# A feed-forward layer whose transposes move to transfers, and whose first token group is held back to the end

## The chip, the cores and the metric

The kernel runs on all 8 cores of one Trainium2 chip. Each core takes one of the 8 sequences (4096 tokens of 1024 features), and the cores don't exchange anything. The metric is the device time of the slowest core in microseconds. A core has TensorE (PE) for matmuls, VectorE (DVE), ScalarE (ACT) and GpSimd (POOL) for the rest, and SyncE (SP), whose queue issues nearly all transfers here. Each engine works through its own instructions in the order in which the program lists them, and waits for the others by semaphores.

## The reference, cut to what matters

```python
x = x + layernorm(attn(layernorm(x)))   # a selective scan over time, state 256
x = x + layernorm(ffn(layernorm(x)))

def ffn(x):                              # x: tokens x 1024
    h = bit_linear(x, w1)                # activations to 8 bits by token, weights to -1, 0, 1; 1024 -> 4096
    h = conv1d(h, conv_w, pad=(1, 1)) + conv_b   # depthwise over time, 3 taps
    h = silu(h)
    return bit_linear(h, w2)             # again quantized by token; 4096 -> 1024
```

Every token's row is divided by its own largest magnitude and rounded before each of the two linear layers. The second quantization needs the maximum over all 4096 hidden features of a token, so W2 of a token can only begin when all its hidden features are there.

## The kernel before, in words

A first phase (to about 310 us) computes the attention half for 32 groups of 128 tokens and stores its result x2 in memory. The change lies in the second phase, the FFN.

The FFN runs over `NF` = 8 tiles of 512 tokens, each with 32 chunks of 128 hidden features. The loop over `n` goes through 256 such chunks (slot `n`, tile `f1 = n // 32`, slot of the tile `s1 = n % 32`), and in the same pass W2 follows `LAG` + 32 = 38 slots behind: `m = n - 38` is a quarter of the hidden features' pieces of a tile, in steps of 4 chunks by 128 tokens. So a slot holds eight W1 matmuls for chunk `n` (`w1_mm`, line 721) and eight W2 matmuls for piece `m` (`w2_mm`, line 850); eight pieces make one output group `Gx`, of which there are 32 (`NG`), each accumulated in one of two PSUM pairs. The program order of the loop is written out by hand, and is the order on each engine. Slots 0 to 37 have no W2, slots 256 on have no W1.

Per chunk ScalarE evacuates W1's result to `hp` (`evac`, L727) and computes one tap (`tap1`, L746) and, for two chunks at once, SiLU (`silu`, L772). VectorE does the other taps (`conv0` L753, `conv2` L760, `conv1` L765), running maxima (`minmax`, L780) and, for the tile before, the multiply and round of one piece (`quant_mul` L833, `quant_rnd` L839), one slot ahead of the W2 that reads the piece. The hidden values live in a ring `h4` of 72 chunks. At the start of a tile the maxima are combined, transposed on TensorE, turned into scales and broadcast (`absmax_comb`, `absmax_T` L797, `scales`, `bcast` L817 and L820).

Beside this the input groups of the next tile are normalized and quantized, one group each eight slots, by the slot's remainder `r`: GpSimd centres (`ln3_center`, L406), ScalarE squares and VectorE takes the maximum (L411), small instructions follow, ScalarE scales (L435), and VectorE writes the rounded bf16 rows `xqmB` (`quant_x`, L440). With `r == 5` TensorE transposes the eight 128x128 blocks into a PSUM bank (`quant_T`, L447) and with `r == 6` ScalarE copies them to `xqT` (`quant_Tev`, L452), which W1 of the next tile reads: its first `w1_mm` waits for the last group (`a_t2`). The first four groups are done so in the first phase already. During the first tile ScalarE and GpSimd also finish W2's ternary weights (L540, L533).

The convolution needs a token's right neighbour, so the hidden rows of a tile are shifted by one: row 0 of output group 0 belongs to no token (it is left out by `rows`), and the last token, 4095, is left over. Its hidden values are made by `last_hidden` as a single column `hxq`, and `last_mm` (line 953) multiplies it by all of W2 in 64 matmuls with one column of weights, after all others. An output group ends with `fin_stats` on VectorE (L880 to L883), `fin_chain` on GpSimd (L896 to L901), `fin_apply` on ScalarE (L907), the residual add on GpSimd (L911), and `fin_store`. The residual rows are loaded two groups ahead in two buffers `x2r`.

Of the kernel before, what the change touches and what calls it, by code (L numbers as in the profile page):

```python
# [78 lines left out]
def build_program():  # L79
# [98 lines left out]
    with st_:  # L178
# [276 lines left out]


# [415 lines left out]
        def fin_stats(Gx):
            np_ = 1 if Gx == NG else 128
            pb = pairW2[Gx % 2]
            for j in range(12):
                sc("bnF", j)
            c0 = col[("bnF", 0)]
            sc("mF", 0), sc("mF", 1)
            c1 = col[("mF", 0)]
# [273 lines left out]
```

How the kernel before makes its waits and increments, by code:

```python
    def wait(self, en, *toks):  # L47
        for s, v in self.fresh(en, toks):
            self.q[en].append(lambda e, S, s=s, v=v: e.wait_ge(S[s], v))
# [1 line left out]
    def op(self, en, f, *toks, inc=True, attach=True):  # L51
        need = self.fresh(en, toks)
        on = need.pop() if need and attach and en != "t" else None
        for s, v in need:
            self.q[en].append(lambda e, S, s=s, v=v: e.wait_ge(S[s], v))
        sem = self.OWN[en] if inc else None
        if inc:
            self.cnt[sem] = self.cnt.get(sem, 0) + 1
        def emit(e, S):
            i = f(e)
            if on:
                i = i.wait_op(S[on[0]], on[1], "sem-ge")
            if sem:
                i.then_inc(S[sem], 1)
        self.q[en].append(emit)
        return (sem, self.cnt[sem]) if inc else None
# [1 line left out]
    def dma(self, en, out, in_, sem, *toks):  # L69
        self.wait(en, *toks, (sem, self.cnt.get(sem, 0)))
        self.cnt[sem] = self.cnt.get(sem, 0) + 16
        self.q[en].append(lambda e, S: e.dma_start(out=out, in_=in_).then_inc(S[sem], 16))
        return (sem, self.cnt[sem])
```

## Time and profile before

| | |
|---|---|
| median of 3 runs | 1317.0 us (1315.3 to 1319.3) |
| profiled execution: its time, its span | 1316.7 us, 1315.2 us |
| cores, in the profiled execution | 1308.8 to 1315.2 us, granted clock 0.948 to 0.970 |
| busy: PE, DVE, ACT, POOL | 89%, 84%, 65%, 32% of the span |
| FFN | from about 315 us on; W1 ends at 1214 us, W2 at 1306 us |

The profile is that of the slowest core (core 5). Its times are microseconds from the first instruction of the span; a row of instructions gives start, duration, engine and line, what is written and read, and in brackets the idle time before it with what ended it. Matmuls are pipelined, so the sum of their durations is more than their time: it is the starts of two neighbouring rows that tell how long a batch took. The granted clock is 1.00 for 2.4 GHz and 0.50 for 1.2 GHz.

### The profile page before, as it was taken

What the parts mean: (1) busy time and instruction counts of PE and PEld (TensorE: products, weight loads), DVE (VectorE), ACT (ScalarE), POOL (GpSimd) and SP (SyncE); (2) the same over time, 40 slices, a digit from 0 to 9 for tenths busy, and PEclk for the clock granted to TensorE, in tenths of its full rate; (3) what the DMA queues carried; (4) which work ended last, traced back from release to release, by engine and by line L of the source; (5) the groups of instructions that cost most, each with busy time, mean ns of one, the idle gap of its engine ahead of it and who ended that gap; (6) DMA issues with size and microseconds to landing.
All of it is one profiled execution on the core that took longest, in us unless ns stands there. A gap on an engine that the chain in (4) does not pass through costs nothing.

```text
span 1315.2 us, 18619 instructions; the slowest of 8 cores (1308.8 to 1315.2 us)
## 1 busy us (share of the span) xinstructions
PE 1168.4 (89%) x6184; PEld 603.1 (46%) x6184; DVE 1106.9 (84%) x2302; ACT 855.1 (65%) x1131; POOL 419.2 (32%) x654
## 2 busy tenths in 40 slices
...
GB/s 206 319 331 218 186 256 292 311 310 185 207 198 44 46 39 75 49 48 50 80 49 65 49 49 49 54 76 48 65 49 49 49 51 47 33 33 33 63 67 33
DMA packets 40099, 146.51 MB, mean 111 GB/s; under 512 B 4804, under 2 KB 4804, under 8 KB 39748
## 3 DMA queue, kind: packets, MB, share of 16 engines
q1 hardware_dynamic: 39572, 142.69, 33.8%
...
q8 instruction: 51, 0.84, 0.2%
...
HBM read 114.36 MB, written 33.55 MB: 112 GB/s over the span
## 4 chain that ended last, share of the span: by engine, by line
PE 69%; DVE 16%; ACT 5%; DMA 4%; SPq 2%; issue 2%; POOL 1%; POOLq 0%; DVEq 0%; ACTq 0%
PE pF L850 32%; PE pO L721 27%; DMA stg<-w1T 4%; PE pF L326 4%; SPq L72 2%; DVE h L760 2%; PE pO L372 2%; DVE xs L393 1%; DVE h L765 1%; DVE hsc L356 1%; PE pF L953 1%; DVE h L753 1%; PE pT L447 1%; DVE accP L780 1%; DVE ysb L361 1%
## 5 line engine op out<-in xcount | busy, mean ns | idle before, releaser
L850 PE MATMUL pF<-w2q,h 128*128 128x512 fp8e4 x2048 | 480.1, 380 | 1.8 <-DVE h L839 1.8
L721 PE MATMUL pO<-xqT,w1q 128*128 128x512 bf16 x1792 | 427.1, 382 | 5.6 <-ACT xqT L452 5.6
L850 PEld LDWEIGHTS pF<-w2q,h 128*128 128x128 bf16 x2048 | 200.6, 98 | 241.8 <-issue 4.6
L727 ACT ACTIVATE hp<-pO 128x512 bf16<-128x512 f32 x224 | 133.6, 596 | 218.8 <-PE pO L721 217.4
L721 PEld LDWEIGHTS pO<-xqT,w1q 128*128 128x128 fp8e4 x1792 | 175.2, 98 | 213.8 <-issue 10.8
L760 DVE SCALAR_TENSOR_TENSOR h<-hp,cwt,h 128x512 bf16<-128x512 bf16 x256 | 202.8, 792 | 0.7
L746 ACT ACTIVATE bt<-hp,cwt 128x512 bf16<-128x512 bf16 x256 | 183.9, 718 | 6.1
L772 ACT ACTIVATE h<-h 128x1024 bf16<-128x1024 bf16 x128 | 134.9, 1054 | 76.1 <-DVE h L765 75.7
L833 DVE TENSOR_TENSOR h<-h,bc 128x512 bf16<-128x512 bf16 x256 | 151.0, 590 | 0.0
L896 POOL TENSOR_SCALAR sm<-sm 128x1 f32<-128x1 f32 (+1 forms) x33 | 17.2, 522 | 376.6 <-DVE sm L883 376.6
L765 DVE TENSOR_TENSOR h<-h,bt 128x512 bf16<-128x512 bf16 x256 | 115.6, 452 | 14.7 <-ACT bt L746 1.3
L753 DVE TENSOR_SCALAR h<-hp,cwt,cbt 128x512 bf16<-128x512 bf16 x256 | 111.9, 437 | 15.2 <-ACT hp L727 14.7
L911 POOL TENSOR_TENSOR yev<-yev,x2r 128x1024 f32<-128x1024 f32 (+1 forms) x33 | 78.1, 2368 | 45.4 <-ACT yev L907 45.4
L721 PE MATMUL pF<-xqT,w1q 128*128 128x512 bf16 x256 | 66.6, 412 | 29.2 <-ACT hp L727 25.4
L780 DVE TENSOR_TENSOR accN<-accN,h 128x1024 bf16<-128x1024 bf16 x120 | 92.0, 767 | 0.0
L907 ACT ACTIVATE yev<-pF,sm 128x1024 f32<-128x1024 f32 (+1 forms) x33 | 39.6, 1200 | 78.6 <-POOL sm L901 78.6
L780 DVE TENSOR_TENSOR accP<-accP,h 128x1024 bf16<-128x1024 bf16 x120 | 82.1, 684 | 0.1
L741 POOL COPY hs<-hp 128x8 bf16<-128x8 bf16 x64 | 25.8, 403 | 167.4 <-ACT hp L727 167.4
L326 PE MATMUL pF<-selh,wsoT_b 128*128 128x256 bf16 x512 | 70.7, 306 | 4.4 <-ACT selh L319 4.4
L839 DVE TENSOR_SCALAR h<-h 128x512 bf16<-128x512 bf16 x256 | 73.4, 287 | 1.2
L285 PE MATMUL pT<-identb,xn 128*128 128x128 bf16 x256 | 24.6, 253 | 54.1 <-ACT xn L278 52.8
L308 PE MATMUL pF<-xinT,wselT_b 128*128 128x256 bf16 x512 | 65.9, 294 | 0.0
...
## 6 DMA issues: line engine op xcount, KB each, us to landing
stg<-w1T SPq DMA_DIRECT2D x40, 512.0 KB, 15.3
xs<-x SPq DMA_DIRECT2D x32, 512.0 KB, 11.2
stg<-w2T SPq DMA_DIRECT2D x32, 512.0 KB, 9.1
x2c<-xs SPq DMA_DIRECT2D x32, 512.0 KB, 9.0
stgC<-w2T SPq DMA_DIRECT2D x32, 512.0 KB, 5.9
x2r<-x2c SPq DMA_DIRECT2D x31, 512.0 KB, 4.6
out<-yev SPq DMA_DIRECT2D x31, 512.0 KB, 3.0
x2q<-x2c SPq DMA_DIRECT2D x28, 512.0 KB, 3.3
```

Of the source, the lines that this page charges most:

```text
L326: t = P(lambda e, gi_=gi_, m=m, k=k: e.matmul(pF[:, at + 256 * gi_:at + 256 * (gi_ + 1)], wsoT[:, 1024 * k + 128 * m:1024 * k + 128 * (m + ...
L721: p_w1[n] = P(lambda e, k=k: e.matmul(bankW1(n), w1q[:, HD * k + 128 * c:HD * k + 128 * (c + 1)], xT[:, :, k, :], start=(k == 0), stop=(k ...
L727: a_ev[n] = A(lambda e: e.activation(hp3[:, n % 8, 2:514], bankW1(n), AF.Identity), *((v_stt[n - 8], a_bt[n - 8], g_sv[n // 4 - 2]) if n > ...
L746: a_bt[n] = A(lambda e: e.activation(bt[n % 3][:, :], hp3[:, n % 8, 1:513], AF.Identity, scale=cwt[:, 3 * c + 1:3 * c + 2]), v_cv[n - 3] i ...
L753: v_ts[n] = V(lambda e: e.tensor_scalar(H_, hp3[:, n % 8, 0:512], cwt[:, 3 * c:3 * c + 1], cbt[:, c:c + 1], OP.mult, OP.add), p_w2[32 * (o ...
L760: v_stt[n] = V(lambda e: e.scalar_tensor_tensor(H_, hp3[:, n % 8, 2:514], cwt[:, 3 * c + 2:3 * c + 3], H_, OP.mult, OP.add), v_ts[n])
L765: v_cv[n] = V(lambda e: e.tensor_tensor(H_, H_, bt[n % 3][:, :], OP.add), v_stt[n], a_bt[n])
L772: a_si[n] = a_si[n - 1] = A(lambda e: e.activation(pair(n), pair(n), AF.Silu), v_cv[n])
L780: t = V(lambda e: e.tensor_tensor(acc[:, :], acc[:, :], pair(n), o), mm_tok[which], a_si[n])
L833: q_tok[m] = V(lambda e: e.tensor_tensor(piece(m), piece(m), bc2[f % 2][:, 128 * g:128 * (g + 1)].unsqueeze(1).to_broadcast([128, 4, 128]) ...
L850: p_w2[m] = P(lambda e, c=c, jj=jj: e.matmul(pb[:, 512 * jj:512 * (jj + 1)], h43[:, ring(32 * f + c), 128 * g:128 * (g + 1)], w2q[:, D * c ...
L911: g_fo[Gx] = G(lambda e: e.tensor_tensor(Y[0:np_, :], Y[0:np_, :], X2[0:np_, 0:D], OP.add), x2_ld[Gx], a_fa[Gx])
```

## The change

Three things change in the FFN.

- The quantized groups of the next tile are transposed by a transfer from `xqmB` to `xqT` (`turn_x`, issued by SyncE), with `r == 5`; `quant_T` and `quant_Tev` are gone from the loop.
- The groups come every seven slots (`s1 // 7`, `s1 % 7`), so the fourth one's transfer is issued in slot 26 of the tile; before, its transposes stood in slot 29 and their evacuation in slot 30.
- The rounded pieces of output group 0 go to a buffer `held` of their own instead of back to the ring. Their W2 matmuls are left out of slots 38 to 45 and follow after all others, as group 32. The last token's column is written into row 0 of each held chunk, the row that belonged to no token, so `last_mm` is gone and group 32 has 128 rows: token 4095 and tokens 0 to 126. Its scale for rows 1 on is saved by `hold_scale`; loads and stores take three pieces of rows. The end (`fin_end`) works in halves of 512 columns, with the residual add on VectorE and six stores. There is one `x2r` buffer, loaded one group ahead, and no memset of it.

The diff, cut to its core:

```diff
-    def dma(self, en, out, in_, sem, *toks):
+    def dma(self, en, out, in_, sem, *toks, turn=False):
         self.wait(en, *toks, (sem, self.cnt.get(sem, 0)))
         self.cnt[sem] = self.cnt.get(sem, 0) + 16
-        self.q[en].append(lambda e, S: e.dma_start(out=out, in_=in_).then_inc(S[sem], 16))
+        kind = {"transpose": True} if turn else {}
+        self.q[en].append(lambda e, S: e.dma_start(out=out, in_=in_, **kind).then_inc(S[sem], 16))
...
-    hxq = sb("hxq", 32, BF16)
+    held = sb("held", 32 * 128, BF16)
-    x2r = [sb("x2r%d" % k, D, F32) for k in range(2)]
+    x2r = sb("x2r", D, F32)
...
+        def turn_x(gi, dst, xqm, *toks):
+
+            p_t2[gi] = a_t2[gi] = q.dma("sy", dst.rearrange("p (k t) -> p k t", k=8), xqm[:, :],
+                                        "tx", v_xq[gi], *toks, turn=True)
...
         def quant_rnd(m):
-            v_q[m] = V(lambda e: e.tensor_scalar(piece(m), piece(m), RC, -RC, OP.add, OP.add),
+            dst = held3[:, 4 * m:4 * m + 4, :] if m < 8 else piece(m)
+            v_q[m] = V(lambda e: e.tensor_scalar(dst, piece(m), RC, -RC, OP.add, OP.add),
                        q_tok[m])
...
         def w2_mm(m):
+
             f, g, j = m // 32, (m % 32) // 8, m % 8
             Gx = m // 8
             pb = pairW2[Gx % 2]
-            q.wait("t", v_q[m], *(v_w2q[4 * j:4 * j + 4] if m < 8 else ()),
-                   a_fa[Gx - 2] if Gx >= 2 and j == 0 else None)
+            q.wait("t", v_q[m] if Gx < NG else v_hxq[0],
+                   *(v_w2q[4 * j:4 * j + 4] if Gx == 1 else ()),
+                   a_fa[Gx - 2] if Gx >= 3 and j == 0 else None)
             for c in range(4 * j, 4 * j + 4):
+                hid = (held3[:, c, :] if Gx == NG else
+                       h43[:, ring(32 * f + c), 128 * g:128 * (g + 1)])
                 for jj in range(2):
-                    p_w2[m] = P(lambda e, c=c, jj=jj: e.matmul(
-                        pb[:, 512 * jj:512 * (jj + 1)],
-                        h43[:, ring(32 * f + c), 128 * g:128 * (g + 1)],
+                    p_w2[m] = P(lambda e, c=c, jj=jj, hid=hid: e.matmul(
+                        pb[:, 512 * jj:512 * (jj + 1)], hid,
                         w2q[:, D * c + 512 * jj:D * c + 512 * (jj + 1)],
                         start=(c == 0), stop=(c == 31)), inc=(c == 4 * j + 3 and jj == 1))
...
         def rows(Gx):
 
-            if Gx == 0:
-                return 1, 128, 0
             if Gx == NG:
-                return 0, 1, T_TOK - 1
-            return 0, 128, 128 * Gx - 1
+                return [(0, 1, T_TOK - 1), (1, 113, 0), (113, 128, 112)]
+            return [(0, 128, 128 * Gx - 1)]
 
         def load_x2(Gx):
             if Gx > NG:
                 return
-            p0, p1, r0 = rows(Gx)
-            x2_ld[Gx] = q.dma("sy", x2r[Gx % 2][p0:p1, 0:D], x2_h[r0:r0 + p1 - p0, :],
-                              "x2l%d" % (Gx % 2), g_fo[Gx - 2] if Gx >= 2 else fin_ready[0],
-                              v_x2z[0])
+            x2_ld[Gx] = [q.dma("sy", x2r[p0:p1, 0:D], x2_h[r0:r0 + p1 - p0, :],
+                               "x2l%d" % k, g_fo[Gx - 1] if Gx >= 2 else fin_ready[0])
+                         for k, (p0, p1, r0) in enumerate(rows(Gx))]
...
+        def fin_end():
+
+            Gx, k = NG, NG % 2
+            pb, Y, X2 = pairW2[k], yev[k], x2r
+            toks = []
+            for n in range(2):
+                h = slice(512 * n, 512 * (n + 1))
+                toks.append(A(lambda e, h=h: e.activation(
+                    Y[:, h], pb[:, h], AF.Identity, bias=sc("bF", k), scale=sc("rF", k)),
+                    *d_out[Gx - 2], g_fc[Gx]))
+            for n in range(2):
+                h = slice(512 * n, 512 * (n + 1))
+                t = V(lambda e, h=h: e.tensor_tensor(Y[:, h], Y[:, h], X2[:, h], OP.add),
+                      *x2_ld[Gx], toks[n])
+                for i, (p0, p1, r0) in enumerate(rows(Gx)):
+                    q.dma("sy", out_h[r0:r0 + p1 - p0, h], Y[p0:p1, h], "oe%d" % (3 * n + i), t)
...
+        def hold_scale():
+            v_lastg[0] = V(lambda e: e.tensor_copy(sc("g2x"), cols4("g2", 0)[:, 0:1]), v_g2[0])
...
-            v_hxq[0] = V(lambda e: e.tensor_scalar(hxq[:, :], X0, -RC, None, OP.add), t2)
-
-        def last_mm():
-            pb = pairW2[NG % 2]
-            q.wait("t", v_hxq[0], a_fa[NG - 2])
-            for c in range(32):
-                for jj in range(2):
-                    p_last[0] = P(lambda e, c=c, jj=jj: e.matmul(
-                        pb[0:1, 512 * jj:512 * (jj + 1)], hxq[:, c:c + 1],
-                        w2q[:, D * c + 512 * jj:D * c + 512 * (jj + 1)],
-                        start=(c == 0), stop=(c == 31)), inc=(c == 31 and jj == 1))
-
-        fin_ready, v_x2z = [None], [None]
+            v_hxq[0] = V(lambda e: e.tensor_scalar(held3[:, :, 0], X0, -RC, None, OP.add), t2, v_q[7])
...
-            if 0 <= m < NW:
+            if 8 <= m < NW + 8:
                 w2_mm(m)
-            if m == NW:
-                last_mm()
 
             if 0 <= n - 1 < NW:
...
-            gq, r = 4 + n // 8, n % 8
-            if gq < NG:
+            gq, r = 4 + 4 * f1 + s1 // 7, s1 % 7
+            if gq < NG and s1 < 28:
                 if r == 0:
...
                 if r == 5:
-                    quant_T(gq, xqmB, pT1b, pT1_free)
-                if r == 6:
-                    quant_Tev(gq, xqT[gq // 4 % 2][:, D * (gq % 4):D * (gq % 4 + 1)], pT1b, pT1_free,
-                              *((p_w1[32 * (gq // 4 - 2) + 31],) if gq >= 8 else d_x2[NG - 2:NG]))
+                    turn_x(gq, xqT[gq // 4 % 2][:, D * (gq % 4):D * (gq % 4 + 1)], xqmB,
+                           *((p_w1[32 * (gq // 4 - 2) + 31],) if gq >= 8 else d_x2[NG - 2:NG]))
...
             if s1 == 3 and 1 <= f1 <= NF:
                 scales(f1 - 1)
+                if f1 == 1:
+                    hold_scale()
...
             if n == 31:
                 q.wait("v", v_w2q[31], *kw_free, *d_x2[NG - 5:NG])
                 q.wait("sy", *done_a, v_x2[NG - 1], p_o[NG - 1])
-                v_x2z[0] = V(lambda e: e.memset(x2r[0][0:1, :], 0.0))
             if n == 32:
-                for Gx in range(2):
-                    load_x2(Gx)
+                load_x2(1)
 
...
-            if m >= 8 and m % 8 == 0 and m // 8 - 1 < NG:
+            if m >= 16 and m % 8 == 0 and m // 8 - 1 < NG:
                 fin_stats(m // 8 - 1)
                 fin_chain(m // 8 - 1)
-            if m >= 10 and m % 8 == 2 and (m - 10) // 8 < NG:
+            if m >= 18 and m % 8 == 2 and (m - 10) // 8 < NG:
                 fin_apply((m - 10) // 8)
-            if m >= 11 and m % 8 == 3 and (m - 11) // 8 < NG:
+            if m >= 19 and m % 8 == 3 and (m - 11) // 8 < NG:
                 fin_store((m - 11) // 8)
-                load_x2((m - 11) // 8 + 2)
+                load_x2((m - 11) // 8 + 1)
             if n == NW + 2:
                 last_hidden()
         fin_stats(NG)
         fin_chain(NG)
...
         fin_stats(NG)
         fin_chain(NG)
-        fin_apply(NG)
-        fin_store(NG)
+        fin_end()
         q.wait("sy", *q.all())
```

## Rows read from the trace of the kernel before

**Rows 1.** The page: busy time, share of the span and instructions of each engine.
```profile
PE 1168.4 (89%) x6184; PEld 603.1 (46%) x6184; DVE 1106.9 (84%) x2302; ACT 855.1 (65%) x1131; POOL 419.2 (32%) x654
```

**Rows 2.** Stretches of core 5: length, busy PE, PEld, DVE, ACT, POOL, PEclk, DMA.
```profile
345.00:405.00 60.00, 40.77 (x172) 15.41 (x171) 58.67 (x90) 58.36 (x79) 49.65 (x37) 0.94 0.57 176
405.00:427.00 22.00, 13.85 (x56) 5.48 (x57) 19.48 (x40) 18.93 (x27) 6.51 (x8) 0.84 0.08 28
...
470.90:1214.00 743.10, 740.05 (x3592) 343.36 (x3591) 689.52 (x1515) 465.86 (x638) 234.92 (x329) 1.00 0.16 52
```

**Rows 3.** Timeline of PE: start, duration, line and tiles.
```profile
468.76 0.61 PE L447 MATMUL pT<-identb,xqmB 128*128 128x128 bf16 x8
469.21 1.89 PE L721 MATMUL pO<-xqT,w1q 128*128 128x512 bf16 x8
470.94 1.89 PE L850 MATMUL pF<-w2q,h 128*128 128x512 fp8e4 x8
...
504.19 1.89 PE L721 MATMUL pO<-xqT,w1q 128*128 128x512 bf16 x8
...
532.26 1.89 PE L721 MATMUL pO<-xqT,w1q 128*128 128x512 bf16 x8
```

**Rows 4.** Waits of PE and DVE, 442 to 1214 us: total, times, longest.
```profile
PE pT L797 <- DVE sm L428: 3.0, 5, 0.6
...
DVE h L753 <- ACT hp L727: 14.4, 27, 1.3
DVE sm L411 <- POOL x2q L406: 11.0, 10, 1.1
```

**Rows 5.** Timeline of DVE.
```profile
466.48 0.29 DVE L839 TENSOR_SCALAR h<-h 128x512 bf16<-128x512 bf16 x1
...
469.13 0.29 DVE L839 TENSOR_SCALAR h<-h 128x512 bf16<-128x512 bf16 x1
...
470.93 0.69 DVE L880 BATCH_NORM_STATS2 sm<-pF 128x6 f32<-128x512 f32 x1
...
472.38 0.37 DVE L833 TENSOR_TENSOR h<-h,bc 128x512 bf16<-128x512 bf16 x1
...
508.01 2.52 DVE L833 TENSOR_TENSOR h<-h,bc 128x512 bf16<-128x512 bf16 x1
...
510.98 0.74 DVE L760 SCALAR_TENSOR_TENSOR h<-hp,cwt,h 128x512 bf16<-128x512 bf16 x1
...
518.24 0.75 DVE L440 TENSOR_SCALAR xqmB<-x2q,sm 128x1024 bf16<-128x1024 f32 x1 [0.32 <-ACT x2q L435]
```

**Rows 6.** Groups by line: busy us, mean ns, idle before.
```profile
L452 ACT ACTIVATE xqT<-pT 128x1024 bf16<-128x1024 bf16 x32 | 32.6, 1018 | 2.0 <-PE pT L447 2.0
...
L953 PE MATMUL pF<-w2q,hxq 128*1 128x512 fp8e4 x64 | 14.0, 379 | 0.0
...
L359 DVE TENSOR_TENSOR ch<-bcg,hsc 128x512 f32<-128x512 bf16 x16 | 11.1, 691 | 0.5
```

**Rows 7.** Waits of PE, 314 to 442 us.
```profile
PE pO L721 <- ACT xqT L452: 5.6, 1, 5.6
```

**Rows 8.** A stretch of core 5, columns as in rows 2.
```profile
431.30:438.10 6.80, 5.13 (x19) 3.07 (x20) 4.68 (x14) 4.36 (x6) 0.32 (x2) 0.50 0.29 96
```

**Rows 9.** The chain that ended last: start, duration, what.
```profile
412.24 0.75 DVE xqmB L440
```

**Rows 10.** Timeline, the end.
```profile
1309.81 1.20 ACT L907 ACTIVATE yev<-pF,sm 1x1024 f32<-1x1024 f32 x1 [12.63 <-POOL sm L901]
1311.09 2.33 POOL L911 TENSOR_TENSOR yev<-yev,x2r 1x1024 f32<-1x1024 f32 x1 [1.31 <-ACT yev L907]
```

**Rows 11.** The page: DMA queue, and a transfer's size and time to landing.
```profile
q1 hardware_dynamic: 39572, 142.69, 33.8%
...
out<-yev SPq DMA_DIRECT2D x31, 512.0 KB, 3.0
```

**Rows 12.** Timeline of SP: a store issued.
```profile
1219.87 0.34 SPq L72 DMA_DIRECT2D out<-yev  x1
```

More of the change, by code:

```diff
@@ L187, in build_program @@
         hs4 = hs.ap().rearrange("p (f c t) -> p f c t", f=2, c=32)
+        held3 = held.ap().rearrange("p (c t) -> p c t", c=32)
         h43 = h4.ap().rearrange("p (c t) -> p c t", c=NH4)
@@ L866, in load_x2 @@
                 return
-            p0, p1, r0 = rows(Gx)
-            x2_ld[Gx] = q.dma("sy", x2r[Gx % 2][p0:p1, 0:D], x2_h[r0:r0 + p1 - p0, :],
-                              "x2l%d" % (Gx % 2), g_fo[Gx - 2] if Gx >= 2 else fin_ready[0],
-                              v_x2z[0])
+            x2_ld[Gx] = [q.dma("sy", x2r[p0:p1, 0:D], x2_h[r0:r0 + p1 - p0, :],
+                               "x2l%d" % k, g_fo[Gx - 1] if Gx >= 2 else fin_ready[0])
+                         for k, (p0, p1, r0) in enumerate(rows(Gx))]
         def fin_stats(Gx):
-            np_ = 1 if Gx == NG else 128
             pb = pairW2[Gx % 2]
[L875 to L879, printed above, removed]
-            V(lambda e: e.bn_stats(sm[0:np_, c0:c0 + 6], pb[0:np_, 0:512]),
-              v_fs[Gx - 1] if Gx else None, p_w2[8 * Gx + 7] if Gx < NG else p_last[0])
-            t = V(lambda e: e.bn_stats(sm[0:np_, c0 + 6:c0 + 12], pb[0:np_, 512:1024]))
-            v_fs[Gx] = V(lambda e: e.bn_aggr(sm[0:np_, c1:c1 + 2], sm[0:np_, c0:c0 + 12]), t,
-                         g_fc[Gx - 1] if Gx else None)
+            raw, mv = cols("bnF", 0, 12), cols("mF", 0, 2)
+            V(lambda e: e.bn_stats(raw[:, 0:6], pb[:, 0:512]), v_fs[Gx - 1], p_w2[8 * Gx + 7])
+            t = V(lambda e: e.bn_stats(raw[:, 6:12], pb[:, 512:1024]))
+            v_fs[Gx] = V(lambda e: e.bn_aggr(mv, raw), t, g_fc[Gx - 1])
         def fin_chain(Gx):
-            np_ = 1 if Gx == NG else 128
             f, g, k = Gx // 4, Gx % 4, Gx % 2
-            if Gx == NG:
-                g2 = sc("g2x")[0:1, :]
-            else:
-                g2 = cols4("g2", f)[:, g:g + 1]
-            mF, vF = sc("mF", 0)[0:np_, :], sc("mF", 1)[0:np_, :]
-            eF, rs, rF, bF = [sc(n, k)[0:np_, :] for n in ("eF", "rsF", "rF", "bF")]
-            old = a_fa[Gx - 2] if Gx >= 2 else None
+            g2 = sc("g2x") if Gx == NG else cols4("g2", f)[:, g:g + 1]
+            mF, vF = cols("mF", 0, 2)[:, 0:1], cols("mF", 0, 2)[:, 1:2]
+            eF, rs, rF, bF = [sc(n, k) for n in ("eF", "rsF", "rF", "bF")]
+            old = a_fa[Gx - 2] if Gx >= 3 else None
             t = G(lambda e: e.tensor_scalar(eF, vF, g2, g2, OP.mult, OP.mult), v_fs[Gx],
@@ L903, in fin_apply @@
         def fin_apply(Gx):
-            np_ = 1 if Gx == NG else 128
             k = Gx % 2
-            pb, Y, X2 = pairW2[Gx % 2], yev[Gx % 2], x2r[Gx % 2]
+            pb, Y, X2 = pairW2[Gx % 2], yev[Gx % 2], x2r
             a_fa[Gx] = A(lambda e: e.activation(
-                Y[0:np_, :], pb[0:np_, :], AF.Identity, bias=sc("bF", k)[0:np_, :],
-                scale=sc("rF", k)[0:np_, :]),
-                d_out[Gx - 2] if Gx >= 2 else fin_ready[0], g_fc[Gx])
-            g_fo[Gx] = G(lambda e: e.tensor_tensor(Y[0:np_, :], Y[0:np_, :], X2[0:np_, 0:D], OP.add),
-                         x2_ld[Gx], a_fa[Gx])
```

21 lines of the change are left out of this document (13 added, 8 removed).

## The prediction

> **What bounds the kernel now.** I read the page's busy shares first, then the windows, then the TensorE timeline and the waits of one steady stretch. TensorE is busy most of the span and VectorE is close behind [rows 1], so shares alone decide nothing. The windows [rows 2] split the FFN. In the first tile (345 to 427 us) W1 runs without W2, and TensorE is busy two thirds of the time: there VectorE (58.67 of 60) and ScalarE (58.36 of 60) set the pace. From 470.9 to 1214 us TensorE is busy 740.05 of 743.10 us, at the upper of its two clock levels (granted 1.00, 2.4 GHz). The timeline [rows 3] shows its beat: eight matmuls every 1.73 us, so a slot of eight W1 and eight W2 matmuls takes 3.45 us, and a group's eight transposes put in 0.45 us more (468.76 to 469.21). From 442 to 1214 us TensorE's longest sum of waits is 3.0 us, while VectorE waits for ScalarE's evacuation of W1 (14.4 us over 27 times) and for GpSimd's centring (11.0 us) [rows 4]: VectorE catches up with TensorE about once in each eight slots, and only then. So TensorE is the bound, and VectorE has about 14.4/27 = 0.5 us a group to spare. After W1's end only W2 is left, and TensorE sets the time alone.
>
> **Transposes off TensorE.** 28 groups are quantized in the FFN; each gives up eight transposes on TensorE and one evacuation on ScalarE (1.02 us) [rows 6]. Four lie in the first tile, where TensorE isn't the bound. Of the other 24, the first falls where VectorE still sets the pace, the second is the one at 468.76, counted below with the held group, and 22 lie in the gapless stretch: 22 x 0.445 = 9.8 us off the path.
> The Trainium skill ("VectorE: DVE Perf Modes", section "The three transpose paths") gives 390 ns to a 128x128 transpose on TensorE and 1309 ns to one by DMA, and recommends TensorE where PSUM will do. By 390 ns, 22 groups of eight would be worth 68.6 us, an estimate that the row contradicts; the row's 0.45 us for eight stands. Its 1309 ns would make a group's transfer 10.5 us, if the eight blocks followed one another; no row here shows one.
>
> **The transfer in their place.** The trace has no transposing transfer. From below: a whole 512 KB store lands in 3.0 us [rows 11]. From above: queue 1 took 33.8% of 16 engines' 1315.2 us for 39572 packets, 0.18 us each [rows 11]. The destination is written in 1024 runs of 128 tokens (256 bytes); if each run cost a whole packet, that is 1024 x 0.18 / 16 = 11.5 us, and 14.5 us with the 3.0 us of latency. If it were cut to 16 elements a piece, 8192 pieces would take 92 us. I take under 14.5 us, since 256 bytes is the natural run of this destination. The cover: group 4 of the next tile is ready when L440 ends at 518.99 [rows 5]; at every seven slots this comes three slots earlier, at about 508.6, and the next tile's W1 starts at 532.26 [rows 3]. Less the 0.4 us that the tile now saves, the cover is 23 us. On SyncE the transfer stands right behind the load of the group after next, which waits for the same VectorE instruction, so it adds no wait of its own for the loads and stores behind it; xqmB is read for at most those 14.5 us, and its next writer comes seven slots (24 us) later. ScalarE loses 24 us of evacuations that it had time for, and the bank of the transposes is left to the scale broadcast alone: nothing.
>
> **Every seven slots.** The same work per tile, in 28 slots instead of 32. It puts the maximum (L411) of a group into the slot with the batch statistics, or nearer to GpSimd's residual add. VectorE's instructions are also held up at times: the L833 at 508.01 lasted 2.52 us, the one at 472.38 took 0.37 us [rows 5]. VectorE must stay close enough behind: TensorE's W2 of a slot reads what VectorE rounded in the slot before. Just after that held-up instruction VectorE starts conv2 at 510.98 for a chunk whose W1 began at 504.19 [rows 3, 5], 6.8 us behind; W2 is late from two slots and a half on, 8.6 us. The statistics (1.5 us, 470.93 to 472.38) on top of such a slot make 8.3 us, just within. I take 1.0 us of new stalls in all; bounds 0 and 7 us, the latter where VectorE gives back half of what the path gains (below).
>
> **The held group.** Its 64 W2 matmuls leave slots 38 to 45 and return at the end, where the last token's 64 go (14.0 us [rows 6]): an exchange at equal price, since 64 of the others take 8 x 1.73 = 13.8 us. The gain is at the front, and is not those 13.8 us, because VectorE still rounds those pieces at its own pace. It finishes the first piece of group 1 at 466.48 + 0.29 = 466.77, and the W2 that reads it starts at 470.94 [rows 3, 5]: it can start 4.1 us earlier (transposes of 468.76 included). Can it hold this? The next piece is rounded at 469.13 + 0.29 = 469.42, and TensorE would want it at 466.8 + 3.45 = 470.2: yes. The piece after that comes behind the statistics of group 0 (470.93 to 472.38), which leave this place, as does a residual add. So 4.1 us, bounds 0 (the clock, below) and 4.1.
>
> **First tile.** ScalarE loses four evacuations (4.1 us), one of which ended a wait of 5.6 us of TensorE [rows 7]. VectorE idles only (60 - 58.67) + (22 - 19.48) = 3.9 us there [rows 2], the most that can be won. The wait of 5.6 us itself is mostly beside ScalarE's backlog. The last group's rounded rows (L440 of the chain, ready at 412.99 [rows 9]) come three slots of some 3.1 us earlier, at 403.7, so a transfer of 14.5 us would be in time by 418.2, and W1(32) would start about when it did; a faster one starts it up to 6 us earlier, beside a VectorE that has work. I take 1.5 us, bounds 0 and 3.9.
>
> **The end.** Statistics and GpSimd's chain run as before to 1309.8. Then, before: 1.20 us of ScalarE and 2.33 of GpSimd [rows 10], and a 4 KB store issued at 1313.4 that ends at 1315.2. After: halves of 0.6 us on ScalarE, adds of 0.69 us on VectorE (nearest row: L359 at 691 ns [rows 6]), the last done at 1311.8; but six stores of 0.34 us issue each [rows 12], the big second one (112 rows) out at 1312.9, landing 1.8 to 3.0 us later: 1314.7 to 1315.9. I take a loss of 0.3 us, bounds -0.5 and +0.7. The extra scale copy and the lost memset are 0.1 us beside other work.
>
> **The sum.** 9.8 + 4.1 - 1.0 + 1.5 - 0.3 = 14.1 us. The profiled execution took 1316.7 us (span 1315.2), the median of the runs is 1317.0. 1316.7 - 14.1 = 1302.6 us.
>
> **The rivals.**
> - All of it and more: the first tile gives its 3.9 us and no new stalls appear: 1316.7 - 9.8 - 4.1 - 3.9 = 1298.9. For it: VectorE also loses the statistics and the add of group 0. 12 in 100.
> - VectorE becomes the bound. It has 0.5 us a group to spare and TensorE's period shrinks by 0.445 us; if the new clusters cost it 0.3 us a group, some 7 us come back: 1309.6. For it: 689.5 of 743.1 us busy [rows 2], and its waits for GpSimd are no spare time. Against: waits for GpSimd should shrink, since at three of four groups the centring no longer stands behind a restore. 14 in 100.
> - The clock takes the held group's gain. In slots 38 to 45 TensorE now has half its work. At 431.3 to 438.1, where it waits between batches, it was granted 0.50 (1.2 GHz, half the upper level) for 6.8 us [rows 8]. Once such a stretch falls on the return of W2, 3.4 us are lost, and perhaps a second time: 1306.0. Against: in the first tile W1 alone kept 0.94 of the clock [rows 2]. The Trainium skill ("TensorE: Matmul & The Clock Gate", section "Why this matters for your kernels") warns that an idle gap between bursts brings the lower clock back; the 431.3 row agrees. 10 in 100.
> - Slower: the transposing transfer lands late. One mechanism: each tile's first W1 waits for it, at six boundaries. It decides from a landing of 23 + 14.1/6 = 25.4 us on, where all is eaten; at 29 us (twice my upper value) the cost is 6 x 6 = 36 us, so 1338.6, and at 92 us far worse. For it: nothing in the trace shows such a transfer, and small pieces are dear. 11 in 100.
> - No measurable change (within 0.3%, 4 us, about what a measurement of this kernel can tell): a transfer near 25 us, or clock and VectorE together. 6 in 100.
> - The forecast: 47 in 100.
>
> **How the numbers follow.** 1302.6 is the likeliest. Down to 1296 the range takes in the first rival with 3 us of unknown; up to 1311 it takes in VectorE as the bound and the clock. Outside lie the late transfer and no change, 17 in 100. Faster by over 0.3%: 47 + 12 + 14 + 10 = 83; within: 6; slower: 11.
>
> **What would show it.** Right: no more transposes of xqmB on TensorE in the FFN; W1 and W2 at 1.73 us each without a break from about 467 us to the end of W1; W2 of group 1 some 4 us earlier; the transfer's landing under 15 us, no TensorE wait for it; TensorE's waits still some 3 us; 64 more L850-like matmuls at the end instead of the 128x1 ones. Wrong: TensorE waits for L839 in slots 22 to 24 of a tile (seven-slot clusters), a granted clock of 0.5 around slot 46, W1 that waits for xqT at tile starts, or VectorE with no waits for hp left (then it is the bound). The weakest steps are the landing time and the 4.1 us.

## The result and the profile after

The changed kernel takes 1322.3 us (median), the kernel before 1317.1 us in the same runs: ratio 1.0031, 95% interval 1.0018 to 1.0045. It is 4 us slower, where 14 us less were forecast. Some executions ran slower, with one die's cores at a lower granted clock (here three of ten of the changed kernel and two of ten of the one before): the medians, here and below, are of all executions, the ratios and intervals of the others alone.

The page of the changed kernel: busy times, the queue, and the transposing transfer (from the view of the transfers).

```profile
PE 1134.8 (86%) x5896; PEld 574.5 (43%) x5896; DVE 1107.7 (84%) x2301; ACT 829.7 (63%) x1103; POOL 400.2 (30%) x647
...
q1 hardware_dynamic: 69360, 150.03, 36.9%
...
xqT<-xqmB SPq DMA_TRANSPOSE x28, 4.3
```

In 640 to 1100 us TensorE was busy 457.6 us before and is busy 446.7 us now (windows; the whole spans are no fair comparison with [rows 1], as the granted clock of the first phase differs): it has less to do and waits. The transfer is harmless. It lands after 4.3 us (3.1 to 8.1), and the queue has (69360 - 39572) / 28 = 1064 packets more for each than in [rows 11] (a few of them belong to the other edits). The trace of core 5 has exactly 1024 packets of 256 bytes for each transfer, as the prediction counted, but one takes 0.02 us of an engine, not 0.18.

The waits of the changed kernel in four steady tiles, 640 to 1100 us, TensorE's first, then VectorE's (total, times, longest):

```profile
PE pF L862 <- DVE h L847: 10.2, 8, 1.6
PE pT L804 <- DVE sm L430: 2.5, 4, 0.7
...
DVE sm L413 <- POOL x2q L408: 12.2, 8, 1.9
DVE sm L430 <- POOL sm L425: 6.8, 4, 1.7
```

Before, TensorE never waited for the rounding in these tiles; now it does (L847 is L839 of before), 10.2 us. VectorE's wait for the evacuation of W1 [rows 4], its only spare time, is gone from the list. New is a wait for GpSimd in the small chain of the scales (L430). Two starts of W1, chunk 0 of tiles 3 and 4, give the tile period (timeline of TensorE, changed kernel):

```profile
646.42 0.81 PE L728 MATMUL pO<-xqT,w1q 128*128 128x512 bf16 x3
...
762.55 1.67 PE L728 MATMUL pO<-xqT,w1q 128*128 128x512 bf16 x7
```

116.1 us a tile. Before it was 114.4 us (646.67 to 761.09), and 112.6 us was forecast. Five such tiles cost 8.6 us; on core 5 the first tile is 4.0 us shorter than before (317.10 to 417.68 in place of 314.77 to 419.39), the second 0.3 us shorter, the rest 0.5 us longer, and that leaves a loss of some 5 us.

Where the delay starts, in slots 7 and 8 of a tile (timeline of VectorE and GpSimd, changed kernel):

```profile
677.46 1.19 POOL L408 TENSOR_SCALAR x2q<-x2q,nmean,ones 128x1024 f32<-128x1024 f32 x1
...
678.69 1.22 DVE L413 TENSOR_REDUCE sm<-x2q 128x1 f32<-128x1024 f32 x1 [1.94 <-POOL x2q L408]
...
681.08 2.50 POOL L906 TENSOR_TENSOR yev<-yev,x2r 128x1024 f32<-128x1024 f32 x1 [2.16 <-ACT yev L903]
...
681.28 2.83 DVE L767 SCALAR_TENSOR_TENSOR h<-hp,cwt,h 128x512 bf16<-128x512 bf16 x1
```

VectorE waits 1.94 us for the centring; then the residual add begins as the maximum is over, and conv2 (0.75 us by itself) takes 2.83 us, until the add is done. The same work in the same kernel with eight slots a group (run e1 below):

```profile
669.90 1.38 POOL L408 TENSOR_SCALAR x2q<-x2q,nmean,ones 128x1024 f32<-128x1024 f32 x1
...
671.24 2.35 POOL L906 TENSOR_TENSOR yev<-yev,x2r 128x1024 f32<-128x1024 f32 x1
671.31 1.22 DVE L413 TENSOR_REDUCE sm<-x2q 128x1 f32<-128x1024 f32 x1 [1.10 <-POOL x2q L408]
672.45 1.43 DVE L840 TENSOR_TENSOR h<-h,bc 128x512 bf16<-128x512 bf16 x1
```

Here the add runs beside the maximum, which keeps its 1.22 us, and only 1.0 us of it falls on L840 (0.42 us by itself). The Trainium skill ("GPSIMD Engine Reference", section "Key points") says that GpSimd shares its interfaces to SBUF with VectorE, and that they contend when VectorE's instruction has two inputs from SBUF or runs in a two-port mode. For the first kind the trace agrees: L767 and L840 read two tensors and are held, the reduction L413 reads one and is not. But L442 and L760 read only one tensor and are held as well (below); the trace does not show in which mode an instruction ran, so whether they are the second kind stays open.

What it comes to, where TensorE waits longest (changed kernel, slots 25 and 26 of the tile; GpSimd and VectorE, then TensorE):

```profile
739.18 2.82 POOL L906 TENSOR_TENSOR yev<-yev,x2r 128x1024 f32<-128x1024 f32 x1 [2.87 <-ACT yev L903]
739.71 2.84 DVE L442 TENSOR_SCALAR xqmB<-x2q,sm 128x1024 bf16<-128x1024 f32 x1
...
740.07 1.89 PE L728 MATMUL pO<-xqT,w1q 128*128 128x512 bf16 x8
743.56 1.89 PE L862 MATMUL pF<-w2q,h 128*128 128x512 fp8e4 x8 [1.61 <-DVE h L847]
```

L442 takes 0.75 us by itself [rows 5, there L440]. W2 starts 3.49 us after W1 in place of 1.73. Read slot by slot, the starts of W1 give the whole difference to e1 of 3.5 us a tile: 1.3 us in slots 9 and 10, 0.2 in 18 and 19, 2.1 in 25 and 26. In the last four slots, which have no group, VectorE catches up (in slots 29 to 31 conv2 is 3.7 to 4.4 us behind W1, as in e1), but what TensorE has waited by then is lost.

### The profile page after: what moved, and what is told of

Same layout as the page of the kernel before. It is cut to its first block, busy times and chain, and to the rows that moved or that the text cites. A ratio compares the mean times of both kernels' runs of the same rounds, so it can differ in the third digit from the quotient of the medians.

```text
span 1322.3 us, 18080 instructions; the slowest of 8 cores (1313.7 to 1322.3 us)
## 1 busy us (share of the span) xinstructions
PE 1134.8 (86%) x5896; PEld 574.5 (43%) x5896; DVE 1107.7 (84%) x2301; ACT 829.7 (63%) x1103; POOL 400.2 (30%) x647
## 3 DMA queue, kind: packets, MB, share of 16 engines
q1 hardware_dynamic: 69360, 150.03, 36.9%
## 4 chain that ended last, share of the span: by engine, by line
DVE 36%; PE 33%; ACT 11%; DMA 8%; issue 6%; POOL 3%; SPq 2%; DVEq 0%; POOLq 0%; ACTq 0%
PE pF L862 18%; PE pO L728 12%; DVE h L767 7%; DVE h L772 5%; DMA stg<-w1T 4%; DVE h L760 4%; DVE accP L787 3%; ACT h L779 3%; DMA x2c<-xs 2%; DVE h L840 2%; DVE xqmB L442 2%; SPq L73 2%; DVE sm L413 2%; ACT hp L734 1%; DVE h L847 1%
## 5 line engine op out<-in xcount | busy, mean ns | idle before, releaser
L862 PE MATMUL pF<-w2q,h 128*128 128x512 fp8e4 x1984 | 466.3, 381 | 16.9 <-DVE h L847 16.2
L728 PE MATMUL pO<-xqT,w1q 128*128 128x512 bf16 x1792 | 427.4, 382 | 10.8 <-ACT hp L734 10.8
L862 PEld LDWEIGHTS pF<-w2q,h 128*128 128x128 bf16 x1984 | 192.3, 98 | 256.6 <-issue 34.7
L767 DVE SCALAR_TENSOR_TENSOR h<-hp,cwt,h 128x512 bf16<-128x512 bf16 x256 | 213.2, 833 | 0.7
L760 DVE TENSOR_SCALAR h<-hp,cwt,cbt 128x512 bf16<-128x512 bf16 x256 | 121.0, 473 | 9.7 <-ACT hp L734 9.7
L772 DVE TENSOR_TENSOR h<-h,bt 128x512 bf16<-128x512 bf16 x256 | 116.7, 456 | 14.7 <-ACT bt L753 1.3
L840 DVE TENSOR_TENSOR h<-h,bc 128x512 bf16<-128x512 bf16 x256 | 120.9, 472 | 0.0
L893 POOL TENSOR_SCALAR sm<-sm 128x1 f32<-128x1 f32 x32 | 15.7, 490 | 334.8 <-DVE sm L885 334.8
L787 DVE TENSOR_TENSOR accN<-accN,h 128x1024 bf16<-128x1024 bf16 x120 | 94.6, 788 | 0.0
L906 POOL TENSOR_TENSOR yev<-yev,x2r 128x1024 f32<-128x1024 f32 x31 | 78.1, 2518 | 49.9 <-ACT yev L903 49.7
L787 DVE TENSOR_TENSOR accP<-accP,h 128x1024 bf16<-128x1024 bf16 x120 | 84.7, 706 | 0.1
L903 ACT ACTIVATE yev<-pF,sm 128x1024 f32<-128x1024 f32 x31 | 37.1, 1196 | 65.7 <-POOL sm L898 65.7
L374 PE MATMUL pO<-woutT_b,ysb 128*128 128x512 bf16 x128 | 36.3, 410 | 47.0 <-DVE xs L395 45.0
L847 DVE TENSOR_SCALAR h<-h 128x512 bf16<-128x512 bf16 x248 | 71.5, 288 | 1.2
## 6 DMA issues: line engine op xcount, KB each, us to landing
stg<-w2T SPq DMA_DIRECT2D x32, 512.0 KB, 10.4
```

The source lines that it names most:

```text
L728: p_w1[n] = P(lambda e, k=k: e.matmul(bankW1(n), w1q[:, HD * k + 128 * c:HD * k + 128 * (c + 1)], xT[:, :, k, :], start=(k == 0), stop=(k ...
L760: v_ts[n] = V(lambda e: e.tensor_scalar(H_, hp3[:, n % 8, 0:512], cwt[:, 3 * c:3 * c + 1], cbt[:, c:c + 1], OP.mult, OP.add), p_w2[32 * (o ...
L767: v_stt[n] = V(lambda e: e.scalar_tensor_tensor(H_, hp3[:, n % 8, 2:514], cwt[:, 3 * c + 2:3 * c + 3], H_, OP.mult, OP.add), v_ts[n])
L772: v_cv[n] = V(lambda e: e.tensor_tensor(H_, H_, bt[n % 3][:, :], OP.add), v_stt[n], a_bt[n])
L787: t = V(lambda e: e.tensor_tensor(acc[:, :], acc[:, :], pair(n), o), mm_tok[which], a_si[n])
L840: q_tok[m] = V(lambda e: e.tensor_tensor(piece(m), piece(m), bc2[f % 2][:, 128 * g:128 * (g + 1)].unsqueeze(1).to_broadcast([128, 4, 128]) ...
```

## The experiments

All ratios are to the kernel before on the same chip; 0.0010 is 1.3 us. The times in the expectations count from a kernel before of 1317 us, so it is the ratios that they are held against (on the chips of these runs it took 1313 to 1317 us).

**The three parts, one by one.** e1 is the changed kernel with the old rhythm:

```diff
-            gq, r = 4 + 4 * f1 + s1 // 7, s1 % 7
-            if gq < NG and s1 < 28:
+            gq, r = 4 + n // 8, n % 8
+            if gq < NG:
```

> The changed kernel with the groups quantized every eight slots again; the transfers and the held group stay. Theory 1 (the seven-slot rhythm moves the residual add of GpSimd and the centring away from the maximum of VectorE, so VectorE falls more than 8.6 us behind and TensorE waits): the tile period falls from 116.1 us to 32 x 3.454 + 2.1 = 112.6 us, five tiles give 17 us and the total is 1301 to 1305 us, with hardly a TensorE wait for the rounding. Theory 2 (VectorE has too little to spare once the transposes are gone, in whatever rhythm): the tile period stays at 115 us or more, the total at 1315 or more, and the waits for the rounding stay above 10 us.

Measured: 1300.5 us, ratio 0.9912 (0.9900 to 0.9925), 11.6 us less. Theory 1 holds, also in the period (timeline of TensorE, run e1):

```profile
636.83 1.46 PE L728 MATMUL pO<-xqT,w1q 128*128 128x512 bf16 x6
...
749.45 0.81 PE L728 MATMUL pO<-xqT,w1q 128*128 128x512 bf16 x3
```

112.6 us to a tenth. In 640 to 1100 us TensorE waits 2.5 us in all, none of it for the rounding. No version that leaves nothing out was faster: it is about 12 us under the kernel before and 1.2% under the changed one.

e2 is the kernel before with `turn_x` in place of `quant_T` and `quant_Tev`, eight slots:

```diff
                 if r == 5:
-                    quant_T(gq, xqmB, pT1b, pT1_free)
-                if r == 6:
-                    quant_Tev(gq, xqT[gq // 4 % 2][...], pT1b, pT1_free, ...)
+                    turn_x(gq, xqT[gq // 4 % 2][...], xqmB, ...)
```

> The kernel before with the transposes done by transfers, and nothing else. Theory 1: the tile period falls by four times 0.445 us to 112.6 us, and the first tile by up to 2 us: 1305 to 1308 us in all. Theory 2 (VectorE at its limit, or transfers that disturb): no change within 3 us, 1314 to 1317 us.

Measured: 1303.7 us, ratio 0.9935 (0.9923 to 0.9948), 8.6 us less (6.8 to 10.1), just under the 9 to 12 expected; the tile period is 112.6 us. Theory 2 falls.

e3 is e1 with the opposite edit, transposes back on TensorE, so the held group and the new end alone.

> The kernel before with the held group and the new end, transposes on TensorE, every eight slots. By the prediction 3.7 us from slots 38 to 45 and minus 0.3 us at the end: 1313 to 1314 us. If TensorE's clock takes it at the return of W2: 1317 us. The tile period stays at 114.4 us.

Measured: 1308.0 us, ratio 0.9960 (0.9947 to 0.9972), 5.3 us less with bounds of 3.7 and 7.0: the expected 3.4 us lie just outside. Its return of W2 (timeline of TensorE, run e3, core 4):

```profile
456.38 3.47 PE L728 MATMUL pO<-xqT,w1q 128*128 128x512 bf16 x8 [2.22 <-ACT hp L734]
...
462.22 1.89 PE L862 MATMUL pF<-w2q,h 128*128 128x512 fp8e4 x8 [0.20 <-DVE h L847]
463.94 1.89 PE L728 MATMUL pO<-xqT,w1q 128*128 128x512 bf16 x8
```

The W1 of slot 45 still takes 3.3 us for eight matmuls, then the pace is full: W2 returns as soon as its piece is rounded (the wait before it is 0.20 us), at 1.73 us for eight matmuls.

e4 is the kernel before with the seven-slot lines alone.

> The kernel before with the groups every seven slots, and nothing else. Theory 1: the same clusters on VectorE as in the changed kernel, so a tile period of 116.5 to 118 us (116.1 of the changed kernel, plus up to 1.8 us of transposes) in place of 114.4 us: slower, 1328 to 1340 us. Theory 2 (the rhythm is harmless, VectorE only lacks the time that the transposes gave it): 1315 to 1320 us.

Measured: 1323.7 us, ratio 1.0082 (1.0069 to 1.0095), 10.8 us more. That is the lower edge of theory 1 (11 to 23 us), and theory 2's -2 to +3 is excluded. The tile period is 116.5 us. So without the rhythm the two other parts give 11.6 us; the rhythm takes 10.8 us from the kernel before and 1.0031 / 0.9912 = 1.2%, 15.7 us, from the kernel with the other two. (With both intervals the latter is 1.0 to 1.4%.) The tile periods say the same and say why: the two kernels at seven slots lie at 116.5 and 116.1 us, where TensorE waits for VectorE's rounding (7.2 and 10.2 us in 640 to 1100 us), those at eight at 114.4 and 112.6 us, where it doesn't. So the rhythm costs more where TensorE's tile is shorter.

**Crowding or alignment?** Seven slots change two things: four groups crowd into 28 slots, and each meets the output groups' work (statistics in slots 6, 14, 22, 30; adds in 0, 8, 16, 24) elsewhere. e5 and e6 keep e1's even spacing and shift all groups by a slot:

```diff
-            gq, r = 4 + n // 8, n % 8
-            if gq < NG:
+            gq, r = 4 + (n + 1) // 8, (n + 1) % 8     # e5; group 4's centre is issued in slot 0
+            gq, r = 4 + (n - 1) // 8, (n - 1) % 8     # e6; from n = 1 on
```

> The kernel of run e1 with every group one slot earlier (centre in slots 7, 15, 23, 31, maximum in the slot whose end issues the residual add): the same even spacing of eight slots, but the add of GpSimd now meets the taps instead of the maximum, as it does in slot 8 of the changed kernel. If where the add falls is what costs (alignment): VectorE loses some 2 us a group, TensorE waits for the rounding, tile period 113.5 to 115 us, 1305 to 1315 us in all. If only the crowding of four groups into 28 slots costs (density): as e1, 112.6 us and 1301 us.

> The kernel of run e1 with every group one slot later (centre in slots 1, 9, 17, 25, maximum two slots behind the slot of the add). Alignment: the add meets the taps here too, so 1303 to 1315 us. Density: as e1, 1301 us. The transfer of the last group lands by slot 32 (4.3 us after slot 30), so no wait at tile starts.

Measured: e5 1329.3 us, ratio 1.0107 (1.0089 to 1.0125), the slowest of all, with tiles of 116.6 to 119.0 us (118.2 on average over four of core 5) where the worst expected was 115; e6 1305.6 us, ratio 0.9926 (0.9910 to 0.9941), not to be told from e1 by its time, though its tile period is 113.4 us. Even spacing doesn't save e5, so crowding is not needed for the loss. But "the add meets the taps" doesn't settle the size: e6 loses hardly anything by it, e5 more than expected. The groups of VectorE and GpSimd and the waits before them, over 640 to 1100 us, show where e5 loses it. First e5, then the changed kernel, then e1 (busy us, mean ns, idle before):

```profile
L760 DVE TENSOR_SCALAR h<-hp,cwt,cbt 128x512 bf16<-128x512 bf16 x124 | 83.0, 669 | 0.0
...
L906 POOL TENSOR_TENSOR yev<-yev,x2r 128x1024 f32<-128x1024 f32 x16 | 64.6, 4036 | 40.9 <-ACT yev L903 40.9
...
L413 DVE TENSOR_REDUCE sm<-x2q 128x1 f32<-128x1024 f32 x16 | 19.5, 1220 | 31.1 <-POOL x2q L408 31.1
```

```profile
L767 DVE SCALAR_TENSOR_TENSOR h<-hp,cwt,h 128x512 bf16<-128x512 bf16 x127 | 106.2, 836 | 0.0
...
L840 DVE TENSOR_TENSOR h<-h,bc 128x512 bf16<-128x512 bf16 x126 | 58.8, 467 | 0.0
...
L906 POOL TENSOR_TENSOR yev<-yev,x2r 128x1024 f32<-128x1024 f32 x16 | 41.0, 2564 | 22.8 <-ACT yev L903 22.6
...
L442 DVE TENSOR_SCALAR xqmB<-x2q,sm 128x1024 bf16<-128x1024 f32 x16 | 20.4, 1272 | 0.5
```

```profile
L767 DVE SCALAR_TENSOR_TENSOR h<-hp,cwt,h 128x512 bf16<-128x512 bf16 x131 | 97.5, 744 | 0.0
L840 DVE TENSOR_TENSOR h<-h,bc 128x512 bf16<-128x512 bf16 x131 | 76.3, 582 | 0.0
...
L413 DVE TENSOR_REDUCE sm<-x2q 128x1 f32<-128x1024 f32 x16 | 19.5, 1220 | 17.6 <-POOL x2q L408 17.6
L442 DVE TENSOR_SCALAR xqmB<-x2q,sm 128x1024 bf16<-128x1024 f32 x16 | 12.0, 751 | 2.9 <-ACT x2q L437 2.5
```

In e5 the add is stretched too. One add there, with what VectorE runs beside it (timeline, core 5):

```profile
677.30 0.75 DVE L767 SCALAR_TENSOR_TENSOR h<-hp,cwt,h 128x512 bf16<-128x512 bf16 x1
677.60 3.92 POOL L906 TENSOR_TENSOR yev<-yev,x2r 128x1024 f32<-128x1024 f32 x1 [2.67 <-ACT yev L903]
677.96 0.69 DVE L787 TENSOR_TENSOR accN<-accN,h 128x1024 bf16<-128x1024 bf16 x1
...
678.90 0.42 DVE L840 TENSOR_TENSOR h<-h,bc 128x512 bf16<-128x512 bf16 x1
679.23 2.44 DVE L760 TENSOR_SCALAR h<-hp,cwt,cbt 128x512 bf16<-128x512 bf16 x1
```

The add lasts 1.57 us longer than its 2.35 us, about as long as VectorE takes for L767, L787, L772 and L840, and these keep their time; the next one, L760, is held until the add is done. So one of the two engines is held while the other works, and it isn't always VectorE.

Two kinds of cost add up for VectorE: what it waits for GpSimd, and by how much its instructions outlast their time alone. In e1 the L840 of four tiles outlast 0.41 us each by 22 us in sum, and the wait is 17.6 us: some 41 us with small ones. In the changed kernel conv2 gives 11.6, L840 7, L442 8.4, the minima (L787) 8, L760 3, and the waits 12.2 + 6.8: 58 us. In e5 L760 gives 32.5 and the wait 31.1: 64 us. The order is that of the times, and the 17 us between e1 and the changed kernel are 4.2 us a tile, where the tile periods differ by 3.5. For e6 the same sum is 48 us, between e1's and the changed kernel's as its tile period is: five groups outlast their time alone by 44 us (L767 3, L772 12, L760 8, L840 8, L847 12), 21 us more than in e1, but the wait is only 4.4 us, 13 us less, since with the centring a slot later VectorE hardly waits for it. The sum is an account, and no proof of the cause; for that something has to be taken away.

**GpSimd taken away.** e7 leaves the residual add out of the changed kernel (`g_fo[Gx] = a_fa[Gx]`, output groups 1 to 31 lack x2); e11 does so at eight slots. e8 leaves the centring out of the changed kernel (`g_c[gq] = xq_ld[gq]`, rows are quantized with their mean).

> The changed kernel, seven slots, with the residual add of GpSimd left out for output groups 1 to 31 (their rows lack x2). If the add holding up VectorE's taps is the main cost of the seven-slot rhythm: tile period back to 112.6 to 113 us, 1302 to 1306 us, no wait for the rounding. If the clusters of maximum and statistics are: still 114.5 us or more, 1312 us or more.

> The changed kernel, seven slots, with GpSimd's centring left out (the rows are quantized with their mean in them). If VectorE's waits for the centring (12.2 us in 460 us) and its effect on the taps are the main cost: tile period 112.6 to 113.5 us, 1300 to 1306 us. If the add is: 115 us or more, 1314 us or more.

> The kernel of run e1 (eight slots) without GpSimd's residual add for output groups 1 to 31 (their rows lack x2), the base for the same edit at seven slots, which took 1294 us at a tile period of 111.8 us. Theory 1: the same period of 111.8 us, 1292 to 1296 us: without the add the two rhythms are equal. Rival: eight slots are still better by the 3.5 us a tile, 108.5 us and 1276 us.

Measured: e7 1294.2 us, ratio 0.9846 (0.9828 to 0.9864); e8 1292.0 us, ratio 0.9826 (0.9811 to 0.9842); e11 1294.6 us, ratio 0.9828 (0.9775 to 0.9881). e7 and e11 decide it: without the add the two rhythms have nearly the same tile period (111.8 and 111.6 us) and times that can't be told apart, with it they lie 1.2% apart. So seven slots cost nothing here without GpSimd's add. They don't show that the crowding by itself costs VectorE nothing: TensorE is the bound in both, and in e7 VectorE still waits 10.4 us for the evacuation of W1, room in which a small cost would not show. Of e7 and e8 both readings expected only one to help, and both helped more than expected (20 and 23 us less than the kernel before, where 11 to 15 and 11 to 17 stood): taking either away is enough. In 640 to 1100 us TensorE doesn't wait at all in these three:

```profile
640.00:1100.00 460.00, 460.00 (x2164) 211.33 (x2162) 409.47 (x968) 285.22 (x395) 96.60 (x193) 1.00 0.22 65
```

```profile
640.00:1100.00 460.00, 446.72 (x2077) 200.58 (x2076) 426.89 (x934) 275.53 (x381) 144.90 (x208) 1.00 0.21 62
```

The windows are of e7 and of the changed kernel (columns as in rows 2). VectorE's busy share of 0.93 in the second looks like room to spare; with 19 us of waits for GpSimd beside it there is hardly any.

**The centring on ScalarE.** A version with nothing left out: groups 8 to 31 are centred by ScalarE, at eight slots (e9) and at seven (e10).

```diff
+        def ln3_centre_a(gi, dst, src):
+            g_c[gi] = A(lambda e: e.activation(dst[:, 0:D], src[:, 0:D], AF.Identity,
+                                               bias=nmean[:, gi:gi + 1]),
+                        v_x2[gi], xq_ld[gi], g_nm[gi])
...
-                    ln3_center(gq, x2q[gq % 2], x2q[gq % 2])
+                    (ln3_centre_a if gq >= 8 else ln3_center)(gq, x2q[gq % 2], x2q[gq % 2])
```

> The kernel of run e1 (eight slots) with the centring of groups 8 to 31 done by ScalarE instead of GpSimd, 24 instructions of some 1.2 us; the groups of the first tile stay on GpSimd, since ScalarE is full there. Nothing is left out. If GpSimd's hold on VectorE is what VectorE lacks: VectorE's waits for the centring go, the maximum starts earlier, the tile period falls from 112.6 to about 111.8 us (the value of the run without centring), 1294 to 1298 us in all. If ScalarE's added 1.2 us a group delays the evacuation of W1 instead: 1301 us or more.

> The changed kernel (seven slots) with the same move of the centring to ScalarE. If the seven-slot rhythm costs only through GpSimd: tile period 111.8 to 112.6 us, 1293 to 1300 us, no waits for the rounding. If the rhythm itself (four groups in 28 slots) costs beside this: 114 us or more, 1308 us or more.

Measured: e9 1306.6 us, ratio 0.9911 (0.9878 to 0.9943); e10 1314.5 us, ratio 0.9972 (0.9947 to 0.9997). Neither gave what the first reading of each expected. e9 is no faster than e1 (tile period 113.5 us), e10 wins back half of what the rhythm cost and stays in the range of its rival (115.0 us). The waits of e9 over 640 to 1100 us say why:

```profile
PE pT L810 <- DVE sm L436: 5.9, 4, 1.6
...
DVE sm L419 <- ACT x2q L414: 12.7, 12, 1.1
```

VectorE now waits 12.7 us for ScalarE's centring, where it waited 17.6 us for GpSimd's; the add has come free of the centring and falls onto the taps (mean of L766, the L760 of e1: 660 ns in place of 407), and TensorE waits 1.5 us at each tile start for the maxima. The rival of e9 had the time right and not the reason: neither VectorE nor TensorE waits for an evacuation there. The sum of stretching and waits is 48 us in e9 and 54 us in e10, with tile periods of 113.5 and 115.0 us, in line with the four above. Leaving work out had shown what the time is worth, not that moving it would give it.

**The end.**

> The kernel of run e1 with the end of the kernel before: one instruction of ScalarE, one add of GpSimd, then three stores, instead of halves, adds on VectorE and six stores. The prediction gave the new end a loss of 0.3 us (from -0.5 to 0.7): from the last matmul to the end of the span 9.5 to 10.8 us here, against about 9.9 to 10.4 us in the changed kernel.

Measured, in a single run: from the first statistics of the last group to the end of the span 14.4 us (1290.62 to 1305.0), against 10.0 us in e1 and in the changed kernel and 9.2 us before. The expectation (9.5 to 10.8) was wrong in size. The timeline of SyncE (e12, then the changed kernel) has the reason:

```profile
1298.25 4.94 SPq L73 DMA_DIRECT2D out<-yev  x3
```

```profile
1317.77 2.33 SPq L73 DMA_DIRECT2D out<-yev  x6
```

With one semaphore (`ot0`) the program makes each store wait for the landing of the one before; the new end gives six stores six semaphores and issues them one behind the other. Of the 4.4 us some 2.9 lie behind the add (from its end to the end of the span 6.9 us in e12, 3.9 in the changed kernel), and some 1.5 before it, where the work in halves and the add on VectorE count.

## Why the prediction was wrong

**The step that failed** is the one on every seven slots: "I take 1.0 us of new stalls in all; bounds 0 and 7 us". It measured 15.7 us beside the other two parts, 10.8 us alone. The prediction saw an L833 of 2.52 us (at 508.01) and counted it into the 6.8 us that VectorE was behind. It didn't ask what held it, which is the add (timeline of GpSimd, kernel before):

```profile
507.89 2.35 POOL L911 TENSOR_TENSOR yev<-yev,x2r 128x1024 f32<-128x1024 f32 x1 [1.81 <-ACT yev L907]
```

In the steady tiles before, two adds of four fell on L833 alone, and two ran first beside the maximum, whose time they don't change; at seven slots one of four begins beside the maximum and the others fall on conv2, the minima and L442. The prediction then took the worst slot and added the statistics, 8.3 us against 8.6, as if one slot were hit once. In the changed kernel the hits follow each other within a few slots: statistics, the wait for the centring, the maximum and the add in slots 6 to 8; statistics and maximum, a wait of 1.8 us for GpSimd's small chain (L425) and L442 under an add in slots 22 to 25. Behind them conv2 is 8.5 to 10.5 us behind W1, and stays there for slots. The rival "VectorE becomes the bound" had the mechanism and half the price; against it stood "waits for GpSimd should shrink", where they grew from 8.8 to 19.0 us in 640 to 1100 us, in the slots with a chain of GpSimd just ahead (1.94 us in place of 1.10).

**Transposes off TensorE**: right. Forecast 9.8 us for 22 groups and up to 1.5 us in the first tile; e2 gave 8.6 us (6.8 to 10.1), the tile period fell by the 1.8 us of four times 0.445, and the first tile gave nothing (below).

**The transfer**: right, and better than its bound: 4.3 us against "under 14.5" (in e2 one of each core's 28 took 16.6 to 16.7 us, in the second tile, where nothing waited for it). What was too dear was the packet: with 1024 x 0.02 / 16 = 1.3 us for 0.18's 11.5, and the 3.0 us of latency, its own sum gives 4.3 us. The cover was 19 us in the second tile (issued at 511.2, W1 at 530.3) where 23 were forecast; with eight slots it is 12 us in the steady tiles of e1, still enough.

**The held group**: 3.7 to 4.1 us forecast, 5.3 us measured with an end that cost 0.8, so some 6 us for the front, above the bound of 4.1. The traces agree: from the first W1 of the second tile to the W2 of group 1 it is 51.4 us in the kernel before and 45.3 in e3 (both core 4). W2 returned when VectorE had rounded its piece, as forecast; but the prediction took VectorE's pace as given, and VectorE had the piece ready 2.2 us earlier (47.3 us and 45.1 us after that W1), as its waits on the way fell from 3.6 to 1.1 us: for the broadcast of the scales from 2.1 to 1.1, for the centring from 1.0 to none. In the changed kernel little of this was left, which the prediction named as a sign ("W2 of group 1 some 4 us earlier"): VectorE, with more of the groups' work before slot 46, had the piece ready after 50.3 us, and W2 started after 50.5 us (core 5), 1.1 us earlier than before. The clock rival did occur there once, on the core shown and on none of the other seven (windows):

```profile
468.20:471.60 3.40, 3.40 (x9) 1.20 (x10) 3.30 (x8) 2.46 (x5) 0.00 (x0) 0.50 0.00 0
```

The first W2, behind a wait of 2.26 us, ran at the lower level: 3.36 us for eight matmuls, 1.6 us lost.

**The first tile**: the wait of 5.6 us for `xqT` [rows 7] is gone only with seven slots. With eight, the fourth group is ready so late that W1 waits for its transfer to land (waits of TensorE, run e2, core 5):

```profile
PE pO L727 <- DMA xqT<-xqmB: 5.0, 1, 5.0
```

From the first to the 33rd W1 the changed kernel needs 100.6 us on core 5 where the one before needs 104.6; e1 and e2, with the transfer at eight slots, need 105.5 and 105.2, and e4, with seven slots and no transfer, 100.3. So the 1.5 us forecast for this tile was too little (4.0 us), and all of it belongs to the rhythm, none to the transfer. Seven slots were right for this one tile and wrong from then on: against e1 they win 5 us in it, lose 5 us in the second tile and 3.5 us in each of the next five.

**The end**: forecast a loss of 0.3 (up to 0.7), measured 0.8 us (10.0 against 9.2). By e12 the halves, the adds on VectorE and the separate semaphores together save 4.4 us against the old form with 128 rows.

**The sum without the rhythm** would have been 15.1 us; e1 measured 11.6 (9.9 to 13.2). The first tile, of which 1.5 us were expected and which gave nothing, and the end make 2 us of the difference.
